# Second attention output in two halves of 256 queries, with the third norm's statistics and the output projections in another order

## The reference

```python
# attention with one head of 128, over x: 2 x 512 x 512
qkv = x @ Wqkv + bqkv
attn = softmax(q @ k.T / sqrt(128))
out = attn @ v                       # 2 x 512 x 128
x = layernorm(x + out @ Wo + bo)     # the third norm
# experts: 64 with rank 16, 16 of them per token
scores = x @ Wr.T
gates = softmax of the top 16 scores, 0 for the others
out = ((x @ A) * gates) @ B * 2.0
x = layernorm(x + out)               # the fourth norm
```

## Time and profile before

| what | us |
|---|---|
| median of 3 runs | 517.43 (516.74 to 517.47) |
| the profiled execution | 515.85 |
| its span, first to last instruction | 514.0 |
| TensorE busy in the span | 482.7 (94%) |
| VectorE, ScalarE, GpSimd busy | 375.4, 291.0, 276.3 |
| granted TensorE clock, mean | 0.997 of full speed |

### The profile page before, as it was taken

The page is one execution under the profiler, slowest core; times in us unless marked ns, Lnnn a source line. Parts: engine busy times, 40 slices in busy tenths (PEclk is TensorE's granted clock), DMA queues, the critical chain, the costliest instruction groups (busy, mean ns, idle before and its releaser), DMA issues.

```text
span 514.0 us, 7457 instructions
## 1 busy us (share of the span) xinstructions
PE 482.7 (94%) x2248; PEld 391.7 (76%) x2248; DVE 375.4 (73%) x707; ACT 291.0 (57%) x539; POOL 276.3 (54%) x255
## 2 busy tenths in 40 slices
PE   2488989999999999999999999999998999999995
PEld 1246668888888888888888888888886788888884
DVE  6979889847897887997979964884567946466433
ACT  6879868756655775765665733636586512333021
POOL 4786766776655775766665754756299210110001
PEclk9999999999999999999999999999999999999998
DMA  7664532613323332332433201730000000000011
GB/s 213 215 238 133 154 85 84 181 46 102 98 74 97 102 114 92 106 119 83 124 104 94 71 1 53 248 141 1 1 1 0 2 1 22 22 20 22 1 42 41
DMA packets 21415, 43.01 MB, mean 84 GB/s; under 512 B 3328, under 2 KB 3456, under 8 KB 21120
## 3 DMA queue, kind: packets, MB, share of 16 engines
q1 hardware_dynamic: 21152, 42.16, 26.6%
q0 software_dynamic: 224, 0.38, 0.3%
HBM read 40.42 MB, written 2.10 MB: 83 GB/s over the span
## 4 chain that ended last, share of the span: by engine, by line
PE 84%; DVE 4%; issue 4%; ACT 3%; POOL 1%; ACTq 0%; DVEq 0%; POOLq 0%
PE bank L1114 74%; PE bank L1282 2%; PE bank L1127 2%; PE bank L1402 1%; PE bank L1174 1%; ACT prob L1070 1%; PE bank L1136 1%; DVE rmax L1666 0%; ACT pT_hi L887 0%; PE bank L1162 0%; DVE bn L1620 0%; DVE pT_lo L1459 0%; PE bank L1315 0%; ACT eb_hi L887 0%; PE bank L1171 0%
## 5 line engine op out<-in xcount | busy, mean ns | idle before, releaser
L790 POOL TENSOR_TENSOR wf<-value,scale 128x512 f32<-128x512 f32 x50 | 64.6, 1291 | 70.4 <-DVE value L1491 70.1
L1114 PE MATMUL bank<-x_hi,gu_hi 128*128 128x512 f32 x224 | 88.5, 395 | 0.0
L1114 PE MATMUL bank<-x_lo,gu_hi 128*128 128x512 f32 x224 | 87.3, 390 | 0.0
L1114 PE MATMUL bank<-x_hi,gu_lo 128*128 128x512 f32 x224 | 87.3, 390 | 0.0
L870 POOL TENSOR_TENSOR rstd<-veps,neg_half 128x1 f32<-128x1 f32 x24 | 13.2, 550 | 110.8 <-issue 104.6
L895 ACT ACTIVATE bank<-code 128x512 f32<-128x512 int32 x124 | 68.7, 585 | 0.0
L1455 DVE TENSOR_TENSOR xs<-bank,xs 128x512 f32<-128x512 f32 x56 | 38.5, 687 | 23.9 <-PE bank L1114 23.4
L1469 DVE SCALAR_TENSOR_TENSOR low<-bent,bank 128x512 f32<-128x512 f32 x62 | 42.3, 682 | 12.0 <-ACT bank L895 7.4
L1114 PEld LDWEIGHTS bank<-x_hi,gu_lo 128*128 128x128 f32 x224 | 42.1, 188 | 8.8
L1114 PEld LDWEIGHTS bank<-x_lo,gu_hi 128*128 128x128 f32 x224 | 42.1, 188 | 7.9
L1114 PEld LDWEIGHTS bank<-x_hi,gu_hi 128*128 128x128 f32 x224 | 42.1, 188 | 7.9
(11 more groups left out here) (228 smaller groups left out, 1163.7 us busy)
## 6 DMA issues: line engine op xcount, KB each, us to landing
code<-codes SPq DMA_DIRECT2D x62, 256.0 KB, 2.7
scale<-scales SPq DMA_DIRECT2D x100, 128.0 KB, 3.0
xs<-xT SPq DMA_DIRECT2D x2, 1024.0 KB, 7.4
ea_raw<-ex_A SPq DMA_DIRECT2D x1, 2048.0 KB, 9.7
eb_raw<-ex_B SPq DMA_DIRECT2D x1, 2048.0 KB, 8.7
out<-rows SPq DMA_DIRECT2D x8, 256.0 KB, 2.0
bgu_raw<-loB_gu SPq DMA_DIRECT2D x1, 896.0 KB, 5.8
wqkv_raw<-w_qkv SPq DMA_DIRECT2D x1, 768.0 KB, 4.3
```

The costliest lines, as they stand in the source:

```text
L790: pool.tensor_tensor(w, v, scale[:, i % RING_CODES, :], ALU.mult).then_inc(scaled_done, 1)
L1114: last = nc.tensor.matmul(ps, a, b, start=start and i == 0 and n == 0, stop=stop and i == len(terms) - 1 and n == 2)
```

## The change

The output of the second sequence is computed in two halves of 256 queries: `ot:1.0` into the left half of bank 3, `ot:1.1` into the right half of bank 6 (`ot_part`). Each has 12 matmuls of 256 columns, its own high part and its own remainder. ot:1.0 waits for pturn:1.1 only; ot:1.1 for pturn:1.3 and for the exponentials that read bank 6. wo:4 and wo:5 wait for the first half, wo:6 and wo:7 for the second, and `h` for the remainder of the second, which reads bank 6. On the list, wo:2 goes ahead of pturn:1.3, wo:3 between the halves, turn:2.0 ahead of wo:4, and score:0 and turn:2.1 ahead of wo:6; wo:7 follows h:0.0. VectorE's order is changed by further moves, ScalarE's by one, and GpSimd gets an order of its own. From `ot:0` to `h:0.0` the orders of the engines become:

Before, VectorE's was: ot:0 pturn:1.0 s:1.2 s:1.3 pturn:1.1 wo:0 pturn:1.2 pturn:1.3 wo:1 wo:2 stat:2.0 ot:1 stat:2.1 wo:3 stat:2.2 wo:4 stat:2.3 wo:5 turn:2.0 wo:6 wo:7 score:0 turn:2.1 h:0.0 turn:2.2 score:1 stat:2.4 h:0.1; ScalarE's: ... pturn:1.3 ot:1 norm:2.0 norm:2.1 turn:2.0 norm:2.2 score:0 turn:2.1 turn:2.2 score:1 norm:2.3. The diff:

```diff
--- before.py
+++ after.py
@@ -315,9 +315,9 @@
     down:6.6 xa:1.1 down:6.7 xa:1.2 xa:1.3 fold:1.1 fold:1.2 fold:1.3 ffn:0 ffn:1 mean:0 stat:1.0 stat:1.1 norm:1.0 norm:1.1
     ffn:2 mean:1 stat:1.2 norm:1.2 ffn:3 stat:1.3 norm:1.3 ffn:4 turn:1.0 stat:1.4 turn:1.1 norm:1.4 ffn:5 stat:1.5
     turn:1.2 turn:1.3 norm:1.5 ffn:6 stat:1.6 ffn:7 norm:1.6 turn:1.4 stat:1.7 turn:1.5 qkv:0.0 qkv:0.1 norm:1.7 turn:1.6 qkv:0.2 turn:1.7 s:0.0 s:0.1 vturn:0 qkv:1.0
-    pturn:0.0 s:0.2 s:0.3 pturn:0.1 qkv:1.1 pturn:0.2 qkv:1.2 pturn:0.3 s:1.0 s:1.1 vturn:1 ot:0 pturn:1.0
-    pturn:1.1 s:1.2 s:1.3 wo:0 wo:1 pturn:1.2 pturn:1.3 wo:2 stat:2.0 ot:1 stat:2.1 wo:3 stat:2.2 wo:4
-    norm:2.0 stat:2.3 norm:2.1 wo:5 turn:2.0 norm:2.2 wo:6 wo:7 score:0 turn:2.1 h:0.0 turn:2.2 score:1
+    pturn:0.0 s:0.2 s:0.3 pturn:0.1 qkv:1.1 pturn:0.2 qkv:1.2 pturn:0.3 s:1.0 s:1.1 vturn:1 ot:0.0 pturn:1.0
+    pturn:1.1 s:1.2 s:1.3 wo:0 wo:1 pturn:1.2 stat:2.0 wo:2 pturn:1.3 ot:1.0 norm:2.0 wo:3 stat:2.1 ot:1.1
+    turn:2.0 norm:2.1 wo:4 wo:5 stat:2.2 score:0 turn:2.1 norm:2.2 wo:6 h:0.0 wo:7 stat:2.3 turn:2.2 score:1
     norm:2.3 stat:2.4 h:0.1 hturn:0.0 h:1.0 hturn:0.1 turn:2.3 h:1.1 stat:2.5 stat:3.0 mix:0 hturn:1.0
     score:2 hturn:1.1 h:2.0 h:2.1 norm:2.4 score:3 norm:3.0 hturn:2.0 mix:1 hturn:2.1 turn:2.4 norm:2.5
     norm:3.1 h:3.0 mix:2 stat:3.1 stat:2.6 turn:2.5 h:3.1 stat:3.2 score:4 hturn:3.0 norm:2.6 h:4.0
@@ -604,7 +604,14 @@
         V, T = vector_order(), tensor_order()
         TAIL = tail_order()
         ACT_TAIL = moved(TAIL, ("vturn", 1), ("s", 1, 0))
-        DVE_TAIL = moved(moved(TAIL, ("pturn", 1, 1), ("wo", 0)), ("wo", 1), ("wo", 2))
+        ACT_TAIL = moved(ACT_TAIL, ("score", 0), ("norm", 2, 2))
+        DVE_TAIL = moved(moved(TAIL, ("s", 1, 2), ("pturn", 1, 0)), ("pturn", 1, 1), ("wo", 0))
+        for item, before in ((("stat", 2, 0), ("pturn", 1, 2)), (("wo", 1), ("ot", 1, 0)), (("wo", 2), ("ot", 1, 1)), (("wo", 3), ("turn", 2, 0)),
+                             (("stat", 2, 1), ("wo", 2)), (("stat", 2, 2), ("wo", 4)), (("stat", 2, 3), ("score", 0)),
+                             (("wo", 6), ("turn", 2, 1)), (("wo", 7), ("turn", 2, 1))):
+            DVE_TAIL = moved(DVE_TAIL, item, before)
+        POOL_TAIL = moved(moved(TAIL, ("stat", 2, 0), ("pturn", 1, 1)), ("stat", 2, 1), ("s", 1, 3))
+        OT = [item for item in TAIL if item[0] == "ot"]
         LAST = ("mix", TT - 1)
 
 
@@ -627,6 +634,12 @@
         def slot_free_down(f):
 
             return TT * (group_of(f - RING_H) + 1)
+
+        def ot_part(item):
+
+            b, c = item[1:]
+            cut = slice(c * SEQ // 2, (c + 1) * SEQ // 2) if b else slice(0, SEQ)
+            return cut, bank[6][:, cut] if c else oT_ps[:, cut]
 
         turn_no = {x: i for i, x in enumerate(x for x in TAIL if x[0] in ("turn", "vturn", "pturn", "hturn"))}
         rows_no = {x: i for i, x in enumerate(x for x in TAIL if x[0] in ("ffn", "wo", "mix"))}
@@ -848,7 +861,7 @@
                     pool.wait_ge(whi_done, late_at[item] + 1)
                     pool.tensor_tensor(lo, raw, hi.bitcast(F32), ALU.subtract).then_inc(wlo_done, 1)
 
-            for item in TAIL:
+            for item in POOL_TAIL:
                 if item[0] == "fold" and item[1] == 0:
 
                     o = item[2]
@@ -1079,9 +1092,9 @@
                     copy(pT_hi[:, :, q * P:(q + 1) * P],
                          turn_ps[i % 2][:, :].rearrange("p (k c) -> p k c", k=TPB), turnhi_done)
                 elif kind == "ot":
-                    b = item[1]
-                    act.wait_ge(oT_ready, b + 1)
-                    copy(oT_hi[:, b, :], oT_ps[:, :], oThi_done)
+                    cut, ps = ot_part(item)
+                    act.wait_ge(oT_ready, OT.index(item) + 1)
+                    copy(oT_hi[:, item[1], cut], ps, oThi_done)
                 elif kind == "score":
                     t = item[1]
                     act.wait_ge(top_step, 5 * t + 3)
@@ -1371,22 +1384,26 @@
                     pe.wait_ge(exp_done, n + 1)
                     turn(turn_ps[i % 2], prob[:, n % 2, :]).then_inc(turn_ready, 1)
                 elif kind == "ot":
-                    b = item[1]
-                    i = turn_no[("pturn", b, TPB - 1)]
+                    b, c = item[1:]
+                    cut, ps = ot_part(item)
+                    i = turn_no[("pturn", b, 1 if item == ("ot", 1, 0) else TPB - 1)]
                     pe.wait_ge(turnhi_done, i + 1)
                     pe.wait_ge(turnlo_done, i + 1)
                     pe.wait_ge(qkvhi_done, 3 * NB)
                     pe.wait_ge(qklo_done, 2 * NB)
-                    if b:
-                        pe.wait_ge(oTlo_done, b)
-                    product(oT_ps[:, :], [(v_hi[:, b, k, :], v_lo[:, b, k, :], pT_hi[:, k, :], pT_lo[:, k, :])
-                                          for k in range(TPB)]).then_inc(oT_ready, 1)
+                    if c:
+                        pe.wait_ge(exp_done, TT - 1)
+                    elif b:
+                        pe.wait_ge(oTlo_done, 1)
+                    product(ps, [(v_hi[:, b, k, :], v_lo[:, b, k, :], pT_hi[:, k, cut], pT_lo[:, k, cut])
+                                 for k in range(TPB)]).then_inc(oT_ready, 1)
                 elif kind == "wo":
                     t = item[1]
                     b = t // TPB
                     rows_wait(rows_no[item])
-                    pe.wait_ge(oThi_done, b + 1)
-                    pe.wait_ge(oTlo_done, b + 1)
+                    part = OT.index(("ot", b, t % TPB // 2 if b else 0))
+                    pe.wait_ge(oThi_done, part + 1)
+                    pe.wait_ge(oTlo_done, part + 1)
                     cut = slice((t % TPB) * P, (t % TPB + 1) * P)
                     product(rows_bank(item)[:, :],
                             [(oT_hi[:, b, cut], oT_lo[:, b, cut], wout_hi[:, :], wout_lo[:, :])]).then_inc(wo_ready, 1)
@@ -1406,6 +1423,7 @@
                     t, c = item[1:]
                     tk = slice(t * P, (t + 1) * P)
                     pe.wait_ge(exp_done, TT)
+                    pe.wait_ge(oTlo_done, len(OT))
                     pe.wait_ge(wlo_done, N_ATTN + N_EA)
                     pe.wait_ge(turnhi_done, turn_no[("turn", 2, t)] + 1)
                     pe.wait_ge(turnlo_done, turn_no[("turn", 2, t)] + 1)
@@ -1677,9 +1695,9 @@
                     rest(pT_lo[:, :, cut], turn_ps[i % 2][:, :].rearrange("p (k c) -> p k c", k=TPB),
                         pT_hi[:, :, cut], turnlo_done)
                 elif kind == "ot":
-                    b = item[1]
-                    dve.wait_ge(oThi_done, b + 1)
-                    rest(oT_lo[:, b, :], oT_ps[:, :], oT_hi[:, b, :], oTlo_done)
+                    cut, ps = ot_part(item)
+                    dve.wait_ge(oThi_done, OT.index(item) + 1)
+                    rest(oT_lo[:, item[1], cut], ps, oT_hi[:, item[1], cut], oTlo_done)
                 elif kind == "wo":
 
                     t = item[1]
```

## The result

The changed kernel takes 513.37 us (median of seven runs, 512.85 to 515.62), the kernel before beside it 516.74. The ratio is 0.9937 with a 95% interval of 0.9920 to 0.9955, so 3.3 us less, between 2.3 and 4.1. The forecast was 514.8 with 2.6 us gained. The profiled execution has a span of 511.6 us against 514.0.

A forecast was written before the change was run, and what follows sets the result against it. TensorE was taken to set the end, its only idle time ahead lying in the edited stretch; turn:2.2 moves from 407.28 to 404.65, and 517.43 - 2.6 = 514.8 us. The range goes from 513.3 to 516.8.

The forecast's parts named there:

- What bounds it: TensorE sets the end; its six waits from 387 us on, 3.0 us together, lie in the edited stretch.
- Half products: Attention output as 24 matmuls of 256 columns at 0.12 us: 2.9 us against 2.8, 1.44 a half.
- The order step by step: Start times from s:1.2's maximum to turn:2.2, which comes at 404.65 instead of 407.28.
- VectorE as the new bound: VectorE has no gap from 394.3 on; search at 402.6, turn:2.2 waits 0.7 us for norm:2.2.
- GpSimd's queue: Power for norm:2.0 at 393.8; 5 us of weight remainders and bias additions follow, needed after 400 us.
- The sum: At turn:2.2, 407.28 - 404.65 = 2.6 us gained, passing through to the end.
- The price of 0.22: Rival 2: weight loads not hidden at 256 columns, 0.22 us each; gain 0.85, 516.6 us; chance 0.10.
- the slower rival: Rival 3: matmuls narrower than a bank run at full fp32 rate, 0.43 us for 256 columns; 521.0 us; chance 0.05.
- Giving it back at hturn:0.1: Rival 4: hturn:0.1, or norm:2.3 behind score:1, holds TensorE; some 1.2 us of gain goes, 516.0; chance 0.10.
- That the order does not bite: Rival 5: norm:2.1 held on POOL behind its bias addition, eviction chain no earlier; 517.3 us; chance 0.07.
- The base: The median of 517.43 us, spreading by 0.7, from which the 2.6 us were taken.

The follow-up runs named there:

- the quarters: Changed kernel with each half product issued as two groups of 128 columns, 48 matmuls instead of 24; 515.69 us, ratio 0.9987 to the kernel before.
- the extra statistic: Changed kernel with one VectorE statistic taken twice ahead of stat:2.2, the second result unused; 514.19 us, ratio 0.9946 to the kernel before.
- the normalization first: Changed kernel with norm:2.2 ahead of score:0's exponential on ScalarE; 513.46 us, ratio 0.9941 to the kernel before.
- the kernel by the list: Changed kernel with GpSimd back in the list's order, its two statistics behind all weight remainders and bias additions; 516.95 us, ratio 1.0007 to the kernel before.
- stat:2.3 late: Changed kernel with VectorE's stat:2.3 behind score:0's search instead of ahead of it; 512.41 us, ratio 0.9921 to the kernel before.
- an extra statistic there: The kernel with stat:2.3 behind score:0's search, with tile 2's statistic taken twice on VectorE; 514.21 us, ratio 0.9954 to the kernel before.
- the order only: Changed kernel's new orders with the second attention output whole (512 columns, one bank); 515.78 us, ratio 0.9978 to the kernel before.

## Why the prediction was right

By its own steps, with 0.2 us taken off the changed kernel's times:

- **What bounds it.** TensorE's 3.0 us of waits between 387 and 405 us were the only ones to be won behind 387 us, and from turn:2.2 to the end the two traces agree (106.72 and 106.85 us). What was gained by turn:2.2 stayed gained.
- **Half products.** I took 0.12 us a matmul, and 0.119 was measured. From start to start the halves took 1.51 and 1.52 us (392.74 to 394.25, 395.27 to 396.79) instead of 1.44, 0.2 us more than the whole output (2.84, 394.20 to 397.04) instead of the 0.1 of the forecast. Their evictions were priced at 0.40 and 0.35 and took 0.39 and 0.33. The row of 128 columns was the right one to choose, though I did not see why: its 0.10 was near a floor (0.112 in the quarters) that stands just under the price of 256 columns. The rule of the Trainium skill ("TensorE: Matmul & The Clock Gate", Part 3) that a load overlaps matmuls only with other row groups would have given an estimated 0.22, and the trace contradicts it at 256 columns too.
- **The order step by step.** The forecast comes first, the measured time in brackets: pturn:1.2 390.8 (measured 390.8), pturn:1.3 392.2 (392.15), the second half 395.2 (395.05), turn:2.0 396.65 (396.6), score:0 398.55 (398.5), the search 402.6 (402.55), turn:2.2 404.65 (404.55). No step is off by more than 0.15. The waits were sized less well: from the last matmul before it, the second half waited 0.3 us where 0.4 was forecast, and turn:2.2 0.6 where 0.7 was.
- **VectorE as the new bound.** This is shown by the extra statistic (+0.6) and by the moved one (-0.6). The wait of turn:2.2 on the normalization is there too, but with the normalization first it goes without help from VectorE; only from score:1 on does VectorE's queue keep 0.3 of these 0.6 us.
- **GpSimd's queue.** I costed the four pieces that come behind the early power at nothing, and took that power as needed for turn:2.0. No wait of TensorE on these pieces shows, and the kernel by the list shows what it costs without the early power: 3.0 us.
- **The sum.** 2.6 us forecast, 2.74 up to turn:2.2, 2.6 at the end of the span. The ratio says 3.3 with 2.3 to 4.1, which holds the 2.6 too, so no difference between the two is shown.
- **The rivals.** The price of 0.22 and the slower rival (full fp32 rate) are refuted by the rows of 256 and of 128 columns. Giving it back at hturn:0.1 did not happen, with 0.6 us of room forecast; where a further 0.6 was gained (stat:2.3 late) hturn:0.1 waited 0.08 us, some 0.5 of the gained 0.6 was left at the end, and an extra statistic there cost its full 0.6. That the order does not bite is refuted by the changed kernel itself, 2.7 us earlier at turn:2.2.
- **Where I was off.** The base: I took the difference off a median of 517.43 of three runs, and the later ones lie at 516.1 to 516.7; 0.7 us of the 1.4 between 514.8 and 513.37 is that. The range hung on the same base, and the time lies only 0.1 us above its lower end of 513.3: that it lies inside is in part luck, while the gain of 2.6 us is not. And in the experiment with the order only, I followed one engine's queue past the point where another's had become later (0.8 instead of 1.4).

## What to carry to other kernels

Where several engines run fixed orders, a schedule by hand from start-to-start times of one trace, all four queues at once, gave the place of turn:2.2 here to 0.2 us or better in all kernels but two; following one queue alone gave 0.6 us of error, and a price not measured before (128 columns) 0.4. A wait of the busiest engine is to be followed back through the queue of each engine behind it, a lightly used one too (here a normalization behind GpSimd's power), since the pieces ahead of that power cost 3 us. And when the effect is smaller than the spread of the executions, measure it in the traces from a mark ahead of the change to one behind it.

## What the runs showed of the hardware

A matmul of this type (fp32r operands) with its own load of 128 columns starts 0.112 us after the one before at 128 columns, 0.119 at 256 and 0.228 at 512, all at the granted clock of 1.0 (2.4 GHz): splitting the 512 columns in two costs little (the whole output took 2.84 us, the halves 3.03), splitting them in four nearly doubles the time (5.34 us in the kernel with quarters). ScalarE's copy takes 0.39 us for 256 columns against 0.60 for 512, VectorE's remainder holds its queue for 0.33 against 0.60, so the two halves cost VectorE 0.06 us more than the whole.
